# Triangle-update layers: the finish stage in chunks of 2048 columns, with accumulated moments

## What is computed

```python
xn    = layernorm(x)                                   # over the 64 channels of a token
left  = (xn @ Wl + bl) * sigmoid(xn @ Wlg + blg)       # times a mask in layers 0 and 2
right = (xn @ Wr + br) * sigmoid(xn @ Wrg + brg)
gate  = sigmoid(xn @ Wog + bog)
o     = einsum('bikc,bjkc->bijc', left, right)         # or over the first index, layers 1 and 3
o     = layernorm(o) * w + b                           # over channels, per (i, j)
out   = (o * gate) @ Wo + bo      # layers 0 and 1: the gate before the output product ("gate_first")
out   = (o @ Wo + bo) * gate      # layers 2 and 3: the gate after it
x     = x + out
```

## Time and profile before

| | us |
|---|---|
| median of 3 runs | 2437.58 (2436.82 to 2440.13) |
| the profiled execution | 2443.13 |
| its span, first to last instruction | 2441.1 |
| finish of layer 0, 1, 2, 3 | 185.3, 185.3, 180.5, 163.0 |
| busy over the span: TensorE, VectorE, ScalarE, GpSimd | 2011.7, 2091.0, 1579.3, 1081.9 |

### The profile page before, as it was taken

The page is one execution under the profiler, slowest core; times in us unless marked ns, Lnnn a source line. Parts: engine busy times, 40 slices in busy tenths (PEclk is TensorE's granted clock), DMA queues, the critical chain, the costliest instruction groups (busy, mean ns, idle before and its releaser), DMA issues. The chain is left out here.

```text
span 2441.1 us, 50395 instructions
## 1 busy us (share of the span) xinstructions
PE 2011.7 (82%) x13892; PEld 1388.7 (57%) x13892; DVE 2091.0 (86%) x3053; ACT 1579.3 (65%) x2341; POOL 1081.9 (44%) x804
## 2 busy tenths in 40 slices
PE   4598969477789898977779889897777988989798
PEld 3433959233333698953333388885333338888465
DVE  5699999899979987879979997876998999787676
ACT  2487789554468777754448776764444888686576
POOL 0077839077657200026747782540443770000476
PEclk8799989699999899989999999998999999999899
DMA  8776837789768848489946682839996788394997
GB/s 331 288 244 238 284 116 245 216 253 330 251 188 255 280 137 275 144 336 369 370 171 240 241 281 82 282 112 337 330 345 236 231 246 298 111 304 163 360 420 297
DMA packets 370777, 624.57 MB, mean 256 GB/s; under 512 B 17520, under 2 KB 246896, under 8 KB 354288
## 3 DMA queue, kind: packets, MB, share of 16 engines
q1 hardware_dynamic: 368368, 606.55, 72.4%
q10 hardware_dynamic: 2304, 16.78, 1.6%
HBM read 413.54 MB, written 209.72 MB: 255 GB/s over the span
## 5 line engine op out<-in xcount | busy, mean ns | idle before, releaser
L696 PE MATMUL bank<-whigh,obuf 128*128 128x128 f16 x4096 | 511.3, 228 | 77.4 <-DMA obuf<-XH 41.4
L696 PEld LDWEIGHTS bank<-whigh,obuf 128*128 128x128 f16 x4096 | 469.2, 126 | 84.0 <-issue 58.6
L613 POOL TENSOR_TENSOR LR<-LR 128x1024 f32<-128x1024 f32 x128 | 374.8, 2929 | 313.9 <-ACT LR L604 313.9
L696 PE MATMUL bank<-wlow,obuf 128*128 128x128 f16 x4096 | 510.6, 228 | 0.0
L696 PEld LDWEIGHTS bank<-wlow,obuf 128*128 128x128 f16 x4096 | 469.6, 126 | 0.0
L832 PE MATMUL bank<-LR 128*128 128x256 f32 (+1 forms) x1792 | 378.9, 375 | 30.6 <-DVE LR L761 16.0
L1146 POOL TENSOR_TENSOR LR<-LR,sum 128x512 f32<-128x512 f32 x128 | 208.6, 1638 | 416.0 <-DVE LR L1177 411.5
L832 PEld LDWEIGHTS bank<-LR 128*128 128x128 f32 (+1 forms) x1792 | 321.8, 181 | 85.6 <-ACT obuf L844 20.9
L1068 PE MATMUL bank<-kst,LR 128*128 128x128 f32 x1024 | 167.0, 287 | 160.6 <-POOL LR L1146 96.3
L575 PE MATMUL bank<-LR,cen 128*128 128x512 f32 x512 | 260.9, 635 | 44.3 <-DVE LR L623 41.1
L1068 PEld LDWEIGHTS bank<-kst,LR 128*128 128x128 f32 x1024 | 116.5, 144 | 309.4 <-POOL LR L1146 174.8
(11 more groups left out here) (115 smaller groups left out, 3615.0 us busy)
## 6 DMA issues: line engine op xcount, KB each, us to landing
LR<-XT SPq DMA_DIRECT2D x128, 512.0 KB, 5.3
obuf<-XH SPq DMA_DIRECT2D x128, 512.0 KB, 5.0
LR<-XT SPq DMA_DIRECT2D x64, 1024.0 KB, 9.3
obuf<-XHA SPq DMA_DIRECT2D x128, 512.0 KB, 4.6
XT<-obuf SPq DMA_DIRECT2D x48, 1024.0 KB, 9.5
OS<-obuf SPq DMA_DIRECT2D x24, 2048.0 KB, 8.1
LR<-OS SPq DMA_DIRECT2D x96, 512.0 KB, 8.1
LR<-XH SPq DMA_DIRECT2D x128, 256.0 KB, 6.4
```

Source lines behind the costliest of these rows:

```text
L613: pool.tensor_tensor(yc[k], yc[k], rs[k], ALU.mult).then_inc(normed.s, 1)
L696: last = pe.matmul(bank(g)[:, j * P:(j + 1) * P], tokens, w[:, half * P:(half + 1) * P], start=part == 0, stop=part == 1)
```

## The change

It touches `finish`, and the statistics behind the two early-gate layers.

- The subtraction of the mean (early gate) and the product with the reciprocal deviation are done for a whole chunk of 2048 columns at once. In the early-gate layers GpSimd does both, into four `nrm` buffers instead of two; in the late-gate layers VectorE does the product.
- `nrm` keeps the order (s, c, v) of `OS`. The instruction writes adjacent columns, and each transpose reads 128 columns at a step of 16 (64 bytes). The channels of a tile come out in another order, so the output weights, their vectors, the gate weights and the centering constant are permuted to match (the constants grow from 772 to 900 columns).
- Early gate: the transposes go to four banks by turns, ScalarE scales in place in PSUM, and VectorE's product reads PSUM. The lags change.
- Early gate: `bn_stats` goes. VectorE's add also gives the sum per channel (`accum_out`), and ScalarE gets a Square per tile, shifted by the old mean, with the sum of squares as `accum_out`, seven tiles behind. `prepare` makes mean and variance of the two.
- SyncE reloads `OS` once the chunk is subtracted (early gate) or multiplied (late gate).

```diff
-            nrm = [flat[:, c * COLS:(c + 1) * COLS] for c in (10, 11)]
-            gated = [flat[:, 14 * COLS + c * BANK:14 * COLS + (c + 1) * BANK] for c in range(4)]
+            nrm = [slot(c) for c in ((10, 11, 14, 15) if gate_first else (10, 11))]
...
-            n_v = [o.rearrange("p (v c s) -> p s c v", s=2, c=C) for o in nrm]
+            n_v = [o.rearrange("p (s c v) -> p s c v", s=2, c=C) for o in nrm]
+            n_t = [o.rearrange("p (w v) -> p w v", v=16) for o in nrm]
+            turn_bank = (lambda k: bank((0, 1, 6, 7)[k % 4])) if gate_first else (lambda k: bank(k % 2))
+            consumed = mean_off if gate_first else normalized
...
-            PO, GL, AL, CL, TB, TBA = (3, 3, 5, 6, 0, 0) if gate_first else (2, 4, 0, 6, 5, 4)
+            SL = 7
+            PO, GL, AL, CL, TB, TBA = (3, 0, 2, 0, 0, 0) if gate_first else (2, 6, 0, 8, 5, 4)
...
                     def next_inputs(i, h):
-                        sp.wait_ge(normalized.s, normalized.n + 16 * i + 4 * h + 4)
+                        sp.wait_ge(consumed.s, consumed.n + 4 * i + h + 1)
...
                     def turn(i, k):
-                        pe.wait_ge(normalized.s, normalized.n + tile + 1)
-                        pe.wait_ge(scaled.s, scaled.n + tile - 1)
+                        if q == 0:
+                            pe.wait_ge(normalized.s, normalized.n + 4 * i + h + 1)
+                        if gate_first:
+                            pe.wait_ge(gated_ready.s, gated_ready.n + tile - 3)
+                        else:
+                            pe.wait_ge(scaled.s, scaled.n + tile - 1)
                         for j in range(4):
-                            last = pe.transpose(by_token(bank(k % 2))[:, :, j, :],
-                                                nrm[h % 2][:, (4 * q + j) * P:(4 * q + j + 1) * P], K(K_IDENT))
+                            last = pe.transpose(by_token(turn_bank(k))[:, :, j, :],
+                                                n_t[h % len(nrm)][:, :, 4 * q + j], K(K_IDENT))
...
                     def scale_shift(i, k):
-                            act.activation(aff[k % 4], bank(k % 2), ACT.Identity, bias=vec(V_OB),
+                            act.activation(turn_bank(k), turn_bank(k), ACT.Identity, bias=vec(V_OB),
                                            scale=vec(V_OW)).then_inc(scaled.s, 1)
...
+                    def square(i, k):
+                        h, q = divmod(k, 4)
+                        act.wait_ge(x_ready.s, x_ready.n + 16 * i + k + 1)
+                        act.wait_ge(stats_taken.s, stats_taken.n + 16 * i + k)
+                        act.activation(sum1[:, :, N:2 * N].rearrange("p t (g f) -> p t g f", f=64),
+                                       pair_cols(xo[h % depth], q).rearrange("p (t g) f -> p t g f", t=2),
+                                       ACT.Square, bias=shift,
+                                       accum_out=stats[:, bass.ds(16 * i + k, 1), 1:2].rearrange("p o f -> p (o f)")) \
+                            .then_inc(stats_taken.s, 1)
...
                 def _(pool):
-                    def normalize(i, k):
-                        if k % 4 == 3:
-                            pool.wait_ge(landed[k // 4].s, landed[k // 4].n + 32 * i + 32)
-                            pool.wait_ge(turned.s, turned.n + 16 * i + k - 7)
-                            pool.tensor_tensor(tile_of(n_v, k), tile_of(o_v, k), token(sum1, i, k), ALU.subtract) \
-                                .then_inc(mean_off_pool.s, 1)
-                            pool.wait_ge(mean_off_pool.s, mean_off_pool.n + 4 * i + k // 4 + 1)
-                        else:
-                            pool.wait_ge(mean_off.s, mean_off.n + 12 * i + 3 * (k // 4) + k % 4 + 1)
-                        pool.tensor_tensor(tile_of(n_v, k), tile_of(n_v, k), token(sum2, i, k), ALU.mult) \
-                            .then_inc(normalized.s, 1)
+                    def normalize(i, h):
+                        pool.wait_ge(landed[h].s, landed[h].n + 32 * i + 32)
+                        pool.wait_ge(turned.s, turned.n + 16 * i + 4 * h - 12)
+                        pool.tensor_tensor(n_v[h], o_v[h], token(sum1, i, h), ALU.subtract).then_inc(mean_off.s, 1)
+                        pool.wait_ge(mean_off.s, mean_off.n + 4 * i + h + 1)
+                        pool.tensor_tensor(n_v[h], n_v[h], token(sum2, i, h), ALU.mult).then_inc(normalized.s, 1)
...
                 def _(dve):
-                    def center(i, k):
...
+                    def normalize(i, k):
+                        if k % 4:
                             return
+                        h = k // 4
+                        dve.wait_ge(landed[h].s, landed[h].n + 32 * i + 32)
+                        dve.wait_ge(turned.s, turned.n + 16 * i + k - 4)
+                        dve.tensor_tensor(n_v[h % 2], o_v[h], token(sum2, i, h), ALU.mult).then_inc(normalized.s, 1)
...
                     def gate(i, k):
-                        dve.tensor_tensor(gated[k % 4], aff[k % 4], og[k % 4], ALU.mult).then_inc(gated_ready.s, 1)
+                        dve.tensor_tensor(gated[k % 4], turn_bank(k), og[k % 4], ALU.mult).then_inc(gated_ready.s, 1)
 
                     def add(i, k):
+                            dve.wait_ge(stats_taken.s, stats_taken.n + 16 * i + k - 12)
                         dve.wait_ge(out_projected.s, out_projected.n + 16 * i + k + 1)
                         dve.scalar_tensor_tensor(pair_cols(xo[h % depth], q), tall(bank(4 + k % 2)), vec(V_BO),
-                                                 pair_cols(xi[h], q), ALU.add, ALU.add).then_inc(x_ready.s, 1)
+                                                 pair_cols(xi[h], q), ALU.add, ALU.add,
+                                                 accum_out=stats[:, bass.ds(16 * i + k, 1), 0:1]
+                                                 .rearrange("p o f -> p (o f)")).then_inc(x_ready.s, 1)
...
                     if gate_first:
-                        pipeline(dve, rounds, 16, (center, 0), (gate, GL), (add, AL), (count, CL))
+                        pipeline(dve, rounds, 16, (gate, GL), (add, AL))
```

In `prepare`, behind an early-gate layer:

```diff
-                    dve.bn_aggr(small[:, 0:2], stats[:, :, :].rearrange("p t f -> p (t f)")).then_inc(step.s, 1)
+                    if from_sums:
+                        dve.reduce_sum(total, stats[:, :, 0:1].rearrange("p t o -> p (t o)"),
+                                       mybir.AxisListType.X).then_inc(summed_up.s, 1)
+                        dve.reduce_sum(squared_total, stats[:, :, 1:2].rearrange("p t o -> p (t o)"),
+                                       mybir.AxisListType.X).then_inc(summed_up.s, 1)
+                        dve.wait_ge(summed_up.s, summed_up.n + 1)
+                        dve.tensor_scalar(mean, total, 1.0 / TOKENS, None, ALU.mult).then_inc(step.s, 1)
...
```

More of the change, by code:

```diff
@@ L60 @@
 X_SCALE = 1024.0
+TOKENS = N * N // 2
 W_SCALE = 1024.0
@@ L161, in build @@
         stats = sb("stats", [P, 4 * NCH, 6])
+        shift = small[:, 15:16]
         unscales = [small[:, i:i + 1] for i in (11, 13)]
@@ L217, in build @@
         stats_taken = sem("stats_taken")
+        summed_up = sem("summed_up")
         normalized = sem("normalized")
@@ L327, in on_pe @@
                 if late:
-                    pe.matmul(bank(6)[:, 0:P], K(K_CENTER), wout_w, start=True, stop=True)
+                    pe.matmul(bank(6)[:, 0:P], K(K_CENTER_OUT), wout_w, start=True, stop=True)
                     pe.matmul(bank(7)[:, 0:1], w_out, vec(V_OB), start=True, stop=True).then_inc(late_folded.s, 1)
@@ L493, in prepare @@
             dev, second, logarithm, a, b, cb = (small[:, i:i + 1] for i in range(2, 8))
+            from_sums = number > 0 and LAYERS[number - 1]["gate_first"]
+            total, squared_total = small[:, 8:9], small[:, 9:10]
             with nc.Block() as block:
@@ L513, in _ @@
                 def _(dve):
-                    dve.bn_aggr(small[:, 0:2], stats[:, :, :].rearrange("p t f -> p (t f)")).then_inc(step.s, 1)
+                    if from_sums:
[5 more added lines that the diff above has]
+                        dve.tensor_scalar(mean, total, 1.0 / TOKENS, None, ALU.mult).then_inc(step.s, 1)
+                        dve.tensor_scalar(dev, total, 1.0 / TOKENS, shift, ALU.mult, ALU.add).then_inc(summed_up.s, 1)
+                        dve.wait_ge(summed_up.s, summed_up.n + 3)
+                        dve.scalar_tensor_tensor(second, dev, -1.0, dev, ALU.mult, ALU.mult).then_inc(summed_up.s, 1)
+                        dve.wait_ge(summed_up.s, summed_up.n + 4)
+                        dve.scalar_tensor_tensor(var, squared_total, 1.0 / TOKENS, second, ALU.mult, ALU.add) \
+                            .then_inc(summed_up.s, 1)
+                        dve.wait_ge(summed_up.s, summed_up.n + 5)
+                    else:
+                        dve.bn_aggr(small[:, 0:2], stats[:, :, :].rearrange("p t f -> p (t f)")).then_inc(step.s, 1)
```

(33 more changed lines are left out.)

45 lines of the change are left out of this document (15 added, 30 removed).

## The result

| | before | after |
|---|---|---|
| median of 4 runs each, us | 2438.86 (2436.82 to 2443.3) | 2383.93 (2377.21 to 2385.01) |
| the profiled execution, us | 2443.13 | 2377.21 |
| its span, us | 2441.1 | 2375.4 |

The changed kernel takes 0.9767 of the time (95% interval 0.9744 to 0.979), 54.9 us less by the medians. The forecast was 2400 in a range of 2384 to 2452: the sign was right, the gain was half as large again as forecast, and the median lies 0.07 us under the low end. The profiled execution of after is the fastest of its four, 6.7 us under their median, and that of before lies 4.3 over its own. Between the two profiles there are therefore 65.9 us, of which 11 belong to the choice of executions.

A forecast was written before the change was run, and what follows sets the result against it. VectorE was taken to bound finish 0 to 2 and TensorE finish 3. Terms of -20, -20, -6 and +9 sum to -37: 2406 us for the profile, 2400 for the median, range 2384 to 2452.

The forecast's parts named there:

- what bounded the three stages: Finish 0 to 2 wait for VectorE, busy 180 of 185 us in the first two, 177 of 180.5 in the third.
- Its price: Finish 0 and 1: a 2048-column GpSimd instruction takes 4.5 us, between estimates of 4.1 and 4.7.
- 160.5 for GpSimd: Finish 0 and 1: 147 us of GpSimd instructions, 1 us of start and the last chunk's four tiles make 160.5 us.
- the -20: Finish 0 and 1: each stage falls to 165 us, a change of -20 us each.
- Its DMA term: Finish 1: 59 MB at 414 GB/s is 142 us, 160 with the start.
- the two engines' holding ends: Finish 0 and 1: no VectorE instruction reads two SBUF tensors, so undisturbed prices hold, 0.74 us for the gate product.
- The accumulators: Finish 0 and 1: sums on VectorE's add and ScalarE's Square cost 0.1 us each per tile.
- the strided weight load: All four finishes: TensorE pays 30 ns a transpose, 0.12 us a tile, 7.7 us a stage.
- Rivals B and C: Transposes: strided load doubles (2427 us, chance 0.25), or also stops hiding beside the matmul before it (2455, chance 0.15).
- the DMA term of finish 0: Finish 0: 51 MB at 350 GB/s is 147 us, plus 18 us before refills start, 165 us.
- Finish 2's 174: Finish 2: DMA takes over from VectorE, 57 MB at 350 GB/s is 163 us, + 11 = 174, so -6.
- The range's low end: Whole kernel: GpSimd at 4.1 us an instruction and free strided loads give -53 us, 2384 us.

The follow-up runs named there:

- E7: Changed kernel with the subtraction of the mean in layers 0 and 1 left out, GpSimd only multiplying: 2362.62 us (one run).
- E2: Changed kernel with VectorE's gate product of layers 0 and 1 reading two SBUF tiles instead of PSUM and SBUF: 2494.07 us (one run).
- E3: Changed kernel with the accumulators of layers 0 and 1 undone (bn_stats and bn_aggr back, no Square): 2380.8 us, ratio to before 0.9765.
- E1: Changed kernel with the transposes of all four finish stages reading 128 adjacent columns instead of a step of 16: 2382.0 us, ratio to before 0.976.
- E5: Changed kernel loading one eighth of the low part of layer 2's gate inputs after the first round: 2369.87 us, ratio to before 0.9709.
- E9: Changed kernel with VectorE subtracting the mean by whole chunks in layers 0 and 1, two chunks ahead; GpSimd only multiplies: 2381.16 us, ratio to before 0.9757.
- E8: Kernel before with only the change's accumulators added (no bn_stats in layers 0 and 1), subtraction and product still by tile: 2418.53 us, ratio 0.9911.

## Why the prediction was right or wrong

**Right: what bounded the three stages, and what bounds two of them now.** VectorE was the bound of finish 0 to 2 and came off it. GpSimd is the bound of finish 1: forecast 147 us for its 32 instructions and 160.5 for the stage, measured 147 from the first start (1046.3) to the last end (1193.2) and 162.3; E7 shows that the stage follows it. Its price was forecast from 256-, 512- and 1024-column rows at 4.5 us and is 4.54 with fp32 inputs. The tail behind the last chunk is 15 us instead of 12.4. In the sum, though, finish 1 stood at 165 like finish 0, above both terms that the forecast had for it (160.5 for GpSimd, 160 for DMA); the -22.9 answers to the terms and not to the -20. Its DMA term was too high as well: E7 ends finish 1 in 146.8 us.

**Right: the two engines' holding ends.** The forecast was that undisturbed prices hold because no VectorE instruction of these stages reads two SBUF tensors any more. The gate products take 686 ns in the mean in both rings, and E2 puts the holding back.

**The accumulators.** VectorE's at 0.1 us was right (14 ns on the add and an 83 ns read), ScalarE's at 0.1 was low: its read takes 194. VectorE's busy time was put at 101 and is 87.4, ScalarE's at 137 and is 129.4; neither is a bound, so neither counts. E3 shows that the whole part is worth nothing beside the chunked form.

**Wrong: the strided weight load, +7.7 us in finish 3.** This is one step that failed, a term of the right kind and far too large. The forecast took 30 ns a transpose, between 7 and 51, "because the loads overlap there and fp32 has more to read". The 51 was the lengthening of an fp16 load by its stride, and the fp32 load lengthened by nearly that, 54. But the price lies in the spacing, and that grew by 3 to 5 ns of 108 (E1), under the low end of 7 that the fp16 loads gave. The forecast leaned halfway to the duration; the rows of before with a spacing in them (62 against 55 ns apart) were the ones to go by. Finish 3 lost 0.9 us where 9 were forecast. Rivals B and C, which made the load dearer still, fall with it.

**Wrong: the DMA term of finish 0, 165 us.** The other failed step. It divided 51 MB by 350 GB/s, the rate of a ten-us window, which is 147 us, and added 18 us of start in which nothing was to move. The table of engines for the first 18 us of finish 0, for ten us in its middle and for ten us of finish 2, changed kernel, answers to it:

```profile
486.60:504.60 18.00, 8.24 (x35) 5.21 (x36) 3.44 (x6) 6.62 (x9) 17.78 (x5) 0.63 0.41 129
...
560.00:570.00 10.00, 9.23 (x43) 5.44 (x42) 6.02 (x14) 9.07 (x19) 9.68 (x4) 1.00 1.07 360
...
1690.00:1700.00 10.00, 9.89 (x46) 5.90 (x45) 9.74 (x13) 6.33 (x11) 6.71 (x7) 1.00 1.07 374
```

The start was real: 129 GB/s in it, but that is 2.3 MB, 6.6 us at 350. The whole stage moved 49.3 MB (317 GB/s in 155.4 us) and not 51. With these two alone, and the forecast's own 350, the sum is 18 us and 134 for the other 47.0 MB, 152 us. Nor is 350 a ceiling: the same layers reach 360 and 374 GB/s here, and the rate of layer 0 lies between 337 and 369 from one execution to the next (the table under E7). By E7 the DMAs' floor is about 154. GpSimd's bf16 subtraction, 4.11 us and not 4.5, brings its own bound down to 156, and so the stage ends at 155 to 162 for a forecast of 165. That the profiled execution shows 155.4 is also luck: it is the one with 369 GB/s. Finish 2's 174 was 169, down to 164 in E3. The mechanism there was right (E5), the size 5 to 10 us too high, with 54 MB moved (319 GB/s in 169.0 us) where 57 were forecast.

**The rest.** -2.2 us outside the four stages, where 0 was forecast. Of these 1.9 lie ahead of finish 0, which begins at 488.46 us before and at 486.57 after, and at 487.3 to 492.6 in the runs above. It was not tested apart.

**By the sum.** Against the profiles the terms missed by 9.4, 2.9, 6.1, 8.1 and 2.2 us, all in one direction, 28.7 of the spans' 65.7. Against the medians the miss is 54.9 less 37.6 (from 2437.6 to 2400), 17 us. The range's low end names a lower price for GpSimd and free loads, and no other rate for DMA; with its DMA terms kept (165, 160 and 174) and finish 3 at +1.2 the sum would be about -50, near its -53. So one bound that was read off ten microseconds was given no range of its own, and the result fell just below. That it fell only 0.07 us below is chance: the medians of E1, E3 and E9, whose times are not told apart from the changed kernel's, are 2380.8 to 2382.0.

## What to carry to other kernels

Where VectorE and GpSimd work side by side in SBUF, give the operations with two SBUF inputs to one of them and let the other read PSUM: then long instructions on GpSimd cost their own time only. With 64 short products of two SBUF tensors left on VectorE the same change lost 54 us instead of winning 55 (E2); 16 long subtractions there, two chunks ahead, cost nothing that shows (E9). Price a longer weight load by the spacing of the matmuls around it, not by its duration. Take a DMA rate from a long window and from several executions, and give it a range. When an operation moves to another engine, follow the loop that it closes (producer, transpose, output, the add ahead of it in the list) before adding up busy times: two chunks of lead instead of one were worth 39 us with no instruction changed.

## What was not expected of the hardware

- An fp32 weight load of 128 columns at a step of 64 bytes takes 194 ns where the packed one takes 140, and four transposes take 0.45 us instead of 0.43 to the next group, so nearly all of the 54 ns is hidden.
- GpSimd's subtraction of 2048 columns takes 4111 ns from bf16 (finish 0) and 4546 from fp32 (the same line in finish 1, mean of 16). The forecast had one price for both.
- Removing 43 us of VectorE instructions that read one SBUF tensor made the subtraction 24% and the disturbed product 32% longer (E8, against the earlier trace rows); busy time of an engine in a shared pair does not add up from undisturbed durations.
- With the same transfers and a DMA share of 1.04 to 1.07, the middle of finish 0 ran at 337, 340, 353 or 369 GB/s in four executions, and the stage's length followed; in layer 1 the rate was 420 or 421 in five.
